# One core: last chunk's reciprocal square root by ScalarE and VectorE in parts, identity products first, and new orders for the last chunks

## The reference

```python
xn = _ln(x, ln1_w, ln1_b); sx = _token_shift(xn, state[:, i1])
# five mixes of xn and sx give w (decay), r, k, v and g = silu(... @ Wg.T)
def step(s, rkvw):
    a = k_t[:, :, :, None] * v_t[:, :, None, :]
    out = einsum('bhk,bhkd->bhd', r_t, u * a + s)
    return (a + w_t[:, :, :, None] * s, out)
att = scan(step)                       # over the 64 tokens
m = mean(a4, -1); var = mean((a4 - m) ** 2, -1)      # a4: att by heads
att = ((a4 - m) * rsqrt(var + EPS)).reshape(b, l, E) * gn_w + gn_b
x = x + att * g @ Wo.T
xn2 = _ln(x, ln2_w, ln2_b); sx2 = _token_shift(xn2, state[:, i0])
xk = xn2 + sx2 * ffn_maa_k; xr = xn2 + sx2 * ffn_maa_r
rr = sigmoid(xr @ ffn_Wr.T); kk = square(relu(xk @ ffn_Wk.T))
x = x + rr * (kk @ ffn_Wv.T)
```

## Time and profile before

| | |
|---|---|
| median of 3 runs | 521.8 us (520.06 to 523.4) |
| the profiled execution | 522.14 us, its span 520.3 us |
| mean granted TensorE clock | 0.987 of full |
| TensorE busy | 479.2 us (92%) |
| VectorE busy | 474.4 us (91%) |
| ScalarE busy | 281.7 us (54%) |
| GpSimd busy | 101.6 us (20%) |

### The profile page before, as it was taken

One profiled execution on the slowest core, in us unless ns is written; L12 is line 12 of the kernel. 1 busy time (PEld: TensorE's weight loads), 2 busy tenths in 40 slices (PEclk: granted clock), 3 DMA queues, 4 the chain that ended last, 5 costly groups with the idle time before them and its releaser, 6 DMA issues. The chain is left out here.

```text
span 520.3 us, 6254 instructions
## 1 busy us (share of the span) xinstructions
PE 479.2 (92%) x2200; PEld 284.2 (55%) x2200; DVE 474.4 (91%) x528; ACT 281.7 (54%) x612; POOL 101.6 (20%) x93
## 2 busy tenths in 40 slices
PE   4868889997989999999999999999999999979896
PEld 2555545553456455655556365655555566556475
DVE  2688899979999999999999989999999999999765
ACT  2443575477537664567645844666636552527243
POOL 0001001301331124210430033211531032122020
PEclk9978999999999999999999989999999999999999
DMA  8282473697389616991489435990579439542030
GB/s 265 121 231 52 107 166 85 145 217 151 72 204 230 122 26 167 220 217 19 103 219 242 85 81 139 216 201 1 121 189 220 78 61 227 126 72 71 1 41 30
DMA packets 26999, 69.49 MB, mean 134 GB/s; under 512 B 1624, under 2 KB 19928, under 8 KB 24536
## 3 DMA queue, kind: packets, MB, share of 16 engines
q1 hardware_dynamic: 19720, 54.68, 41.4%
q0 software_dynamic: 7248, 14.42, 16.4%
HBM read 46.28 MB, written 12.19 MB: 112 GB/s over the span
## 5 line engine op out<-in xcount | busy, mean ns | idle before, releaser
L630 DVE TENSOR_TENSOR_SCAN kv<-w_sb,kv 128x512 f32<-128x512 f32 (+2 forms) x144 | 146.6, 1084 | 0.1
L958 PE MATMUL pa<-x,large_sb 128*128 128x512 f32 (+2 forms) x272 | 115.2, 567 | 5.0 <-DVE x L545 2.9
L451 POOL COPY kv<-s_sb 128x32 f32<-128x32 f32 (+2 forms) x36 | 54.6, 1518 | 145.6 <-PE patt L1130 141.4
L958 PEld LDWEIGHTS pa<-x,large_sb 128*128 128x128 f32 x272 | 51.2, 194 | 57.5 <-issue 44.3
L620 DVE TENSOR_TENSOR kv<-vrep,k_sb 128x2016 f32<-128x2016 f32 (+2 forms) x34 | 70.1, 2064 | 3.3 <-issue 3.3
L638 DVE TENSOR_TENSOR kv<-kv,r_sb 128x2048 f32<-128x2048 f32 (+2 forms) x36 | 72.9, 2043 | 0.2
L536 DVE SCALAR_TENSOR_TENSOR x<-pb,vec_sb,sx 128x512 f32<-128x512 f32 (+1 forms) x64 | 42.7, 708 | 6.0 <-PE pb L1002 5.9
L420 POOL DMA_DIRECT2D x<-xn x21 | 20.0, 951 | 111.5 <-DVE x L536 111.5
L1130 PE MATMUL patt<-kv,const_sb 128*32 128x512 f32 (+2 forms) x288 | 34.7, 557 | 0.5 <-DVE kv L638 0.4
L1002 PE MATMUL pb<-th,w_sb 32*128 32x512 f32 (+2 forms) x100 | 33.3, 596 | 1.5 <-DVE x L536 1.5
L1156 PE MATMUL pc<-large_sb,att 128*128 128x256 f32 x120 | 32.0, 390 | 0.0
(11 more groups left out here) (185 smaller groups left out, 824.6 us busy)
## 6 DMA issues: line engine op xcount, KB each, us to landing
vrep<-v_scratch SPq DMA_DIRECT2D x12, 2048.0 KB, 18.5
x<-xn POOLq DMA_DIRECT2D x18, 512.0 KB, 8.3
vrep<-v_scratch SPq DMA_DIRECT2D x4, 1536.0 KB, 10.8
x_tok<-in_x SPq DMA_DIRECT2D x6, 512.0 KB, 10.2
v_scratch<-v_sb SPq DMA_DIRECT2D x12, 256.0 KB
xres<-in_x SPq DMA_DIRECT2D x6, 512.0 KB, 10.7
out<-xres SPq DMA_DIRECT2D x6, 512.0 KB, 5.0
out<-trr POOLq DMA_DIRECT2D x6, 512.0 KB, 8.1
```

Source lines behind the costliest of these rows:

```text
L451: pool.tensor_copy(kv[:, q % 2, :, 0:nb, 0], s0_sb[:, half, G4 * j:G4 * (j + 1), FIRST[c]:FIRST[c] + nb]).then_inc(s0_put, 1)
L630: ins = dve.tensor_tensor_scan(flat, w_sb[:, p, q % HF, 0:nb].rearrange("p b t -> p (b t)"), flat, 0.0, ALU.mult, ALU.add)
L958: ins = pe.matmul(dst[:, m, 0:n], w(a)[:, m * P:(m + 1) * P], src[:, a, :], start=(a == 0), stop=(a == HF - 1))
```

## The change

For the last chunk alone, "rstd" becomes one Sqrt on ScalarE, with its table set loaded by hand ahead of the wait in "sq", and the Exp set loaded again behind it. rstd then holds the square root, and each of the three gates inverts its own 128 columns on VectorE by a reciprocal and waits for it before scaling. The products with Wo of the parts: the identity product comes first, it waits for rstd_ready and no longer for y_ready; part 10 writes patt instead of pc (`product`), so it waits for scaled to reach PARTS, that all gates have read patt, and no longer for "out" 7. `warm` in WO waits for rstd_ready instead of ln_ready and isn't called for k = 10. WARM changes: WO 8 loses its 6 dummies, WO 9 has 4, the 9 of WO 10 are never issued, T2 9 loses 3, RR 9 loses 1, T2 8 gets 1, T2 7 goes from 14 to 13 and RR 7 from 5 to 2. The tails of all five engines get new orders.

```diff
--- before.py
+++ after.py
@@ -45,22 +45,22 @@
               ("s01", 2), ("rd2", 3), ("ad3", 1)]
 SP_ORDER = [("lx", 3), ("vl0", 5), ("vl1", 5), ("sx2", 6), ("vst", 4), ("lr", 5)]
 SUBS = 3
-DVE_TAIL = [("rs1", 7), ("shift2", 6), ("sc2", 7), ("a3", 7), ("mix4", 8), ("sc3", 7), ("rs2", 7), ("rs3", 7),
-            ("rk", 8), ("out", 6), ("a0", 8), ("a1", 8), ("bonus", 8), ("gate", 7), ("sc0", 8), ("rs0", 8),
-            ("sc1", 8), ("a2", 8), ("sc2", 8), ("rs1", 8), ("rs2", 8), ("shift2", 7), ("a3", 8), ("sc3", 8),
-            ("rs3", 8), ("gate", 8), ("out", 7), ("gate", 9), ("gate", 10), ("st2", 8), ("st2", 9),
+DVE_TAIL = [("rs1", 7), ("shift2", 6), ("a3", 7), ("mix4", 8), ("sc2", 7), ("sc3", 7), ("rs2", 7), ("rs3", 7),
+            ("rk", 8), ("out", 6), ("a0", 8), ("sc0", 8), ("bonus", 8), ("gate", 7), ("a1", 8), ("rs0", 8),
+            ("sc1", 8), ("a2", 8), ("rs1", 8), ("sc2", 8), ("rs2", 8), ("shift2", 7), ("a3", 8), ("sc3", 8),
+            ("rs3", 8), ("gate", 8), ("gate", 9), ("out", 7), ("gate", 10), ("st2", 8), ("st2", 9),
             ("nrm2", 8), ("st2", 10), ("nrm2", 9), ("shift2", 8), ("nrm2", 10), ("shift2", 9), ("shift2", 10),
             ("out", 8), ("out", 9), ("out", 10)]
-PE_TAIL = [("WO", 7), ("BO", 8), ("S0", 8), ("T2", 7), ("S1", 8), ("RR", 7), ("S2", 8), ("KK", 7), ("S3", 8),
+PE_TAIL = [("WO", 7), ("BO", 8), ("S0", 8), ("T2", 7), ("S1", 8), ("S2", 8), ("RR", 7), ("KK", 7), ("S3", 8),
            ("VR", 8), ("Y2", 7), ("WO", 8), ("WO", 9), ("WO", 10), ("T2", 8), ("T2", 9), ("RR", 8), ("T2", 10),
-           ("RR", 9), ("KK", 8), ("RR", 10), ("KK", 9), ("KK", 10), ("Y2", 8), ("Y2", 9), ("Y2", 10)]
-ACT_TAIL = [("r", 8), ("w", 8), ("sq", 7), ("rstd", 7), ("st2", 7), ("nrm2", 7), ("xn2", 7), ("tg", 8),
+           ("KK", 8), ("RR", 9), ("RR", 10), ("KK", 9), ("KK", 10), ("Y2", 8), ("Y2", 9), ("Y2", 10)]
+ACT_TAIL = [("w", 8), ("r", 8), ("sq", 7), ("rstd", 7), ("tg", 8), ("st2", 7), ("nrm2", 7), ("xn2", 7),
             ("rr", 7), ("sq", 8), ("kk", 7), ("rstd", 8), ("st2", 8), ("st2", 9), ("st2", 10), ("xn2", 8),
-            ("xn2", 9), ("xn2", 10), ("rr", 8), ("rr", 9), ("rr", 10), ("kk", 8), ("kk", 9), ("kk", 10)]
-POOL_TAIL = [("s02", 7), ("s03", 7), ("s00", 8), ("ad4", 8), ("ay", 6), ("s01", 8), ("s02", 8), ("rd2", 7),
+            ("xn2", 9), ("rr", 8), ("xn2", 10), ("kk", 8), ("rr", 9), ("rr", 10), ("kk", 9), ("kk", 10)]
+POOL_TAIL = [("s02", 7), ("s03", 7), ("s00", 8), ("ad4", 8), ("s01", 8), ("s02", 8), ("ay", 6), ("rd2", 7),
              ("s03", 8), ("ay", 7), ("rd2", 8), ("rd2", 9), ("ay", 8), ("rd2", 10)]
-SP_TAIL = [("vl1", 6), ("sx2", 5), ("lr", 6), ("vst", 7), ("vl0", 7), ("vl1", 7), ("vst", 8), ("sx2", 6),
-           ("vl0", 8), ("lr", 7), ("vl1", 8), ("sx2", 7), ("lr", 8), ("sx2", 8)]
+SP_TAIL = [("vl1", 6), ("sx2", 5), ("vst", 7), ("vl0", 7), ("vl1", 7), ("lr", 6), ("vst", 8), ("vl0", 8),
+           ("sx2", 6), ("vl1", 8), ("lr", 7), ("sx2", 7), ("lr", 8), ("sx2", 8)]
 DVE_HEAD = [("st1", 0), ("nrm1", 0), ("shift", 0), ("mix2", 0), ("mix0", 0), ("cwv", 0), ("mix1", 0),
             ("mix3", 0), ("cs0", 0), ("a0", 0), ("a1", 0), ("rk", 0), ("shift", 1), ("mix4", 0), ("bonus", 0),
             ("sc0", 0), ("sc1", 0), ("rs0", 0), ("rs1", 0), ("mix0", 1), ("a2", 0), ("mix1", 1), ("mix2", 1),
@@ -89,8 +89,8 @@
              ("s03", 1), ("ad0", 3), ("ay", 0), ("s00", 2)]
 SP_HEAD = [("vst", 0), ("lx", 0), ("lr", 0), ("lx", 1), ("lx", 2), ("lx", 3), ("vl0", 0), ("vl1", 0),
            ("vst", 1), ("vl0", 1), ("vl1", 1), ("sx2", 0), ("lx", 4), ("vst", 2), ("lr", 1)]
-WARM = {("KK", 1): 6, ("RR", 7): 5, ("RR", 9): 1, ("T1", 0): 2, ("T2", 2): 6, ("T2", 3): 6, ("T2", 4): 6,
-        ("T2", 5): 6, ("T2", 6): 6, ("T2", 7): 14, ("T2", 9): 3, ("W1", 0): 1, ("WO", 0): 6, ("WO", 8): 6,
+WARM = {("KK", 1): 6, ("RR", 7): 2, ("T1", 0): 2, ("T2", 2): 6, ("T2", 3): 6, ("T2", 4): 6, ("T2", 5): 6,
+        ("T2", 6): 6, ("T2", 7): 13, ("T2", 8): 1, ("W1", 0): 1, ("WO", 0): 6, ("WO", 9): 4, ("WO", 10): 9,
         ("X01", 0): 2}
 LAGS = 6
 ADDED = (0, 1, 3, 4)
@@ -219,7 +219,7 @@
         bonus_put, scaled, y_ready, x2_ready = [sem(n) for n in ("bonus_put", "scaled", "y_ready", "x2_ready")]
         mean2_ready, var2_ready, xhat2_ready, sx2_ready, xk_ready, xr_ready = [sem(n) for n in ("mean2_ready", "var2_ready", "xhat2_ready", "sx2_ready", "xk_ready", "xr_ready")]
         gated, out_ready, u_put, fv_put, ln_put = [sem(n) for n in ("gated", "out_ready", "u_put", "fv_put", "ln_put")]
-        bn_done, bn_summed, moments_ready = [sem(n) for n in ("bn_done", "bn_summed", "moments_ready")]
+        bn_done, bn_summed, moments_ready, inverted = [sem(n) for n in ("bn_done", "bn_summed", "moments_ready", "inverted")]
         bn_done1, bn_summed1, in_spread, spread = [sem(n) for n in ("bn_done1", "bn_summed1", "in_spread", "spread")]
         wv_summed, wv_centered, s0_summed, s0_centered = [sem(n) for n in ("wv_summed", "wv_centered", "s0_summed", "s0_centered")]
         x2_stored, y_added, squared1, squared2 = [sem(n) for n in ("x2_stored", "y_added", "squared1", "squared2")]
@@ -301,7 +301,7 @@
 
         def product(k):
 
-            return pc if k < LAST else (pa, pb, pc)[k - LAST]
+            return pc if k < LAST else (pa, pb, patt)[k - LAST]
 
         def product_tok(k):
             return product(k)[:, :, :].rearrange("p a (t e) -> p (a t) e", e=E)
@@ -641,6 +641,9 @@
 
                 c, at, n = part(k)
                 dve.wait_ge(rstd_ready, c + 1)
+                if c == LAST:
+                    dve.reciprocal(out=rstd[:, span(k)], in_=rstd[:, span(k)]).then_inc(inverted, 1)
+                    dve.wait_ge(inverted, k - LAST + 1)
                 if k >= 1:
 
                     dve.wait_ge(wo_done, ends(k))
@@ -875,6 +878,8 @@
                 act.activation(sg[:, p, :, 0:n], pa[:, :, 0:n], ACT.Silu).then_inc(sg_ready, 1)
 
             def c_sq(c, p):
+                if c == LAST:
+                    act.preload_act_table_set("sqrt_and_others")
                 act.wait_ge(summed, NQ * (c + 1))
                 if c >= 1 and c != LAST:
                     act.wait_ge(y2_done, c)
@@ -886,6 +891,10 @@
                 if c >= 1:
                     act.wait_ge(scaled, c)
                 n = extent(c)[1]
+                if c == LAST:
+                    act.activation(rstd[:, 0:n], product(c)[:, 1, 0:n], ACT.Sqrt, bias=eps_sb[:, 0:1]).then_inc(rstd_ready, 1)
+                    act.preload_act_table_set("exp_and_others")
+                    return
                 act.activation(rstd[:, 0:n], product(c)[:, 1, 0:n], ACT.Ln, bias=eps_sb[:, 0:1]).then_inc(ln_ready, 1)
                 act.wait_ge(ln_ready, c + 1)
                 act.activation(rstd[:, 0:n], rstd[:, 0:n], ACT.Exp, scale=-0.5).then_inc(rstd_ready, 1)
@@ -1143,15 +1152,20 @@
                 ins.then_inc(var_done, 1)
 
             def wo(k, _):
-                warm("WO", k, product(k), ln_ready, part(k)[0] + 1)
+                if k < PARTS - 1:
+                    warm("WO", k, product(k), rstd_ready, part(k)[0] + 1)
                 if k == 0:
                     pe.wait_ge(in_late, 16)
+                pe.wait_ge(res_in, 16 * (part(k)[0] + 1))
+                if k >= LAST:
+                    pe.wait_ge(rstd_ready, LAST + 1)
+                    if k == PARTS - 1:
+                        pe.wait_ge(scaled, PARTS)
+                    pe.matmul(product_tok(k)[:, 0], ident, xres[:, tiles(k)[0], :], start=True, stop=False)
                 pe.wait_ge(y_ready, k + 1)
-                pe.wait_ge(res_in, 16 * (part(k)[0] + 1))
-                if k == PARTS - 1:
-                    pe.wait_ge(gated, LAST)
                 for i, t in enumerate(tiles(k)):
-                    pe.matmul(product_tok(k)[:, i], ident, xres[:, t, :], start=True, stop=False)
+                    if k < LAST:
+                        pe.matmul(product_tok(k)[:, i], ident, xres[:, t, :], start=True, stop=False)
                     for a in range(HF):
                         ins = pe.matmul(product_tok(k)[:, i], att[:, a, t * P:(t + 1) * P], weight("Wo", a), start=False, stop=(a == HF - 1))
                 ins.then_inc(wo_done, 1)
```

## The result

The changed kernel took 525.06 us in the median of 22 runs (521.58 to 532.33), the kernel before, run between them, 522.12 us (518.91 to 525.58). The ratio is 1.0054 with a 95% interval of 1.0033 to 1.0075: 2.8 us slower, 1.7 to 3.9, clear of noise and under 1%. Runs over 1.5% above the fastest of the same kernel, here two of 22 at 532 us, are in no ratio of this text. The forecast was 521.8 us, range 519.6 to 524.2. The method came out as forecast; the new orders around it cost about 3 us that I had put at 0.7.

The account below looks back on a forecast made before the run. VectorE was taken as packed until chunk 8's last read-out, then a chain to xr of part 10 and six products. The 3.1 us gain was used up by orders, reciprocals and TensorE's queue: +0.05 us, forecast 521.8 us, range 519.6 to 524.2.

Parts of the forecast that it names:

- Part 3: Orders before 490 us: most moves cost nothing, one makes the last read-out of chunk 8 0.7 us later.
- one answer, nothing: Most order moves before 490 us: no cost, since data seemed to be there before its user.
- part 4: From 491 us to the end: delays, gates, TensorE's queue and tail summed to +0.05 us, no change.
- Parts 1 and 2: Last chunk: rstd 3.1 us sooner after the square without table loads and Exp; three VectorE reciprocals at 0.9 us each.
- a cheap and an eight-pass reciprocal: Gate reciprocals: cheap, with the wait before shift2 7 covered, 520.4 us, chance 0.27; eight passes, 522.9 us, chance 0.2.
- flat on one side: Reciprocals at or below 0.7 us: third moments wait on WO 10, so the end comes 0.7 us earlier, no more.
- Part 4's tail: After the gates: third moments at 506.0, xr of part 10 about 511.3, products done 517.2 against 517.15 before.
- Part 3, late gate 7: VectorE: sc0 8 ahead of bonus 8 and gate 7 delays the last read-out by 0.7 us, bounds 0 to 1.3.
- Part 3, rd2 7: GpSimd: ay 6's 1.30 us issue now stands before power rd2 7, costing at most 0.3 us.
- The clock rival: TensorE's clock falls at WO 7 or in the tail: 523.4 us for one short fall, 526 to 527 otherwise; chance 0.13.
- one short fall: TensorE's clock at 1.2 GHz for 3.1 us, worth 1.6 us, giving 523.4 us.
- the tail loses its fillers: TensorE's tail loses dummies: six at WO 8, three at T2 9, one at RR 9; named under the clock rival.

Follow-up runs that it names:

- cheap_recip: Changed kernel with each reciprocal replaced by a multiplication by 1, so its output is wrong; ratio 1.0032 to the kernel before.
- sc2_first: Changed kernel with sc2 8 again ahead of rs1 8 on VectorE; ratio 1.0011 to the kernel before.
- wide_a: Changed kernel with a1 8 also ahead of sc0 8, gate 7 later and TensorE's hole before WO 7 wider, unfilled; ratio 1.0075 to the kernel before.
- late_gate7: Kernel before with one VectorE move: sc0 8 ahead of bonus 8 and gate 7, a1 8 behind them; ratio 1.0026 to the kernel before.
- ay6_early: Changed kernel with ay 6 again ahead of s01 8 on GpSimd; ratio 1.0080 to the kernel before.
- tail_dummies: Changed kernel with the dummies of before at RR 7 (5), RR 9 (1) and T2 9 (3), none at T2 8; ratio 1.0046 to the kernel before.
- fill7: Changed kernel with six dummies added ahead of WO 7; ratio 1.0019 to the kernel before.
- Repaired: Changed kernel with sc2 8 ahead of rs1 8, dummies of before at RR 7, T2 9, RR 9, and six ahead of WO 7; ratio 0.9990 to before.
- gate7_first: Changed kernel with bonus 8 and gate 7 again ahead of sc0 8, a1 8 still behind; ratio 1.0078 to the kernel before.

## Why the prediction was wrong

Two steps failed. Part 3 gave the move of rs1 8 ahead of sc2 8 "one answer, nothing", and it cost 0.74 us. The sum of part 4 went on at full clock, with the falls only a rival of chance 0.13, and they cost some 1.5 us in the mean. The rest held, in the tail by luck as well.

**Parts 1 and 2** held: loads in idle time and none between, no drain behind a load (0.01 and 0.02 us to what follows in the earlier trace rows), the reciprocal 0.99 with its wait against 0.9. From the last read-out to the end of the gates I had 12.45 us, measured 12.20. The choice between a cheap and an eight-pass reciprocal hardly mattered, and cheap_recip shows why, by the mechanism of the forecast's "flat on one side": Y2 7 and WO 9's dummies hold WO. I had let the second and third reciprocal eat 1.8 us of the gain; they cost 0.2, and TensorE's queue ate the rest.

**Part 4's tail** came out by two errors that cancel. From the last read-out to the third moments I had 14.55 us, measured 14.01; from there to the last addition 12.1, measured 12.52 at full clock (sc2_first, wide_a). The whole, 26.6 us in the forecast, was 26.55 in both, where before took 27.33.

**Part 3, late gate 7**, priced at 0.7, measured 0.9 (late_gate7). Right.

**Part 3, rd2 7**, priced at 0 to 0.3 for ay 6's issue: wrong in cause and size. It cost 0.74 (sc2_first), by a move that I passed over among those with "one answer, nothing": rs1 8 ahead of sc2 8, which puts a two-input product with 1.27 us to go under the start of the power. Rows of before had the sign of it: GpSimd's powers of this one shape took between 1.04 and 1.83 us, and its copies of the start states, from 380 us on, between 0.24 and 3.46. I read them as rough spans.

**The clock rival** had the right places and nearly the right price for one short fall (1.6; measured 1.45 at WO 7 and 1.26 in the tail) and a wrong chance. I gave it 0.13 because the shorter holes of before had passed. In the tail it came in 8 of 10 profiles, and at WO 7, with the hole that the change makes, in 2 of 6. It should have stood in the sum. The forecast's remark that the tail loses its fillers named the cause, and part 4's sum then went on at full clock. Two of my numbers there were off, and neither matters: 1.67 us and 0.9 more make a hole of 2.6, not 2.9 (measured 2.76), and the long fall of the earlier trace rows ends at 43.5, not 43.75.

**The sum, with what was measured**: the last read-out at full clock +1.73 (109.90 in ay6_early, tail_dummies, cheap_recip and fill7 against 108.17), of which late gate 7 is 0.87, the power 0.74 and the rest unnamed; the method and the new tail orders at full clock -0.8 (26.55 against 27.33); the fall at WO 7 in 2 of 6, +0.5; the fall in the tail in 8 of 10, +1.0. That is +2.4 us; the ratio says +2.8, 1.7 to 3.9. The two last terms come from few profiles. The granted clock of the runs points the same way: 0.984 in the mean of the changed kernel's 20, 0.985 to 0.989 in the groups of runs of before. Repaired, with power and falls taken out, is 0.57 us over before in its profile, and its ratio reaches from -2.0 to +0.9 us.

## What to carry to other kernels

When an order is changed on one engine, look for what it does to TensorE's idle time and put a fall of the clock into the sum wherever a hole grows beyond those that passed at full clock or fillers go; price it from a fall elsewhere in the trace. Check in which instruction of VectorE a small GpSimd operation on the critical chain will now start, whether it has two inputs in SBUF, and how much of it will be left. Where an operation is swapped for a dearer one, look first whether its consumer's queue is busy anyway, since then its price does not matter, and neither does its gain.

## What the runs showed of the hardware

- A reciprocal of 128x128 fp32 on VectorE takes 0.95 us, a multiplication by a constant of the same tile 0.22 us, a factor of 4.3.
- GpSimd's power over 128x4 waits for the end of a VectorE product or scan with two SBUF inputs in which it starts: 2.17 us with 1.27 us of a product to go, 1.43 with 0.60 of a scan, 1.26 with 0.37 of a product. In a product with one input in PSUM it takes 1.04 us. A product that starts 0.1 us behind the power doesn't hold it (1.03 us, gate7_first).
- Relu and Square run on ScalarE under the table set that was loaded for Sqrt (load at 492.85, Square at 497.50, Relu at 498.21, Sqrt at 500.22, with no load between), and a load of 1.28 us can be placed by hand in idle time.
- With TensorE idle for 2.6 to 2.8 us before WO 7 the clock fell there in 2 of 6 profiles, with 4.3 us in 2 of 2, with 1.7 to 1.9 us in 0 of 5, and with the hole filled by dummies in 0 of 4.
- In the tail, where TensorE has no idle stretch over 1 us ahead of the fall, it fell in 8 of 10 profiles with the few dummies of the change, and in 0 of 7 with those of before.
